# Feed-forward matmuls over 512 tokens at a time, with the two hidden weight matrices streamed through a ring of four slices

## The chip, the core and the metric

The kernel runs on one NeuronCore of a Trainium2 chip. A core has five engines that run side by side and meet only through semaphores: TensorE (PE in the profile; its weight loads are PEld), VectorE (DVE), ScalarE (ACT), GpSimd (POOL) and SyncE (SP), which here only issues transfers. The metric is the device time of one execution in microseconds (us); less is better.

## The reference

Eight batches of 512 tokens with 256 features pass through four residual blocks: a state-space layer (called ssm below), a feed-forward, a delta-rule attention (delta below) and the same feed-forward again with the same weights.

```python
def _L0_ffn_ref(x, w1_w, w1_s, w2_w, w2_s, h1_w, h1_s, h2_w, h2_s, w3_w, w3_s):
    h = jax.nn.silu(_tlin(x, w1_w, w1_s)) * _tlin(x, w2_w, w2_s)      # 256 -> 1024
    h = jax.nn.gelu(_tlin(h, h1_w, h1_s), approximate=False)          # 1024 -> 1024
    h = jax.nn.gelu(_tlin(h, h2_w, h2_s), approximate=False)          # 1024 -> 1024
    return _tlin(h, w3_w, w3_s)                                       # 1024 -> 256
...
x = x + ssm(_layernorm(x))
x = x + ffn(_layernorm(x))
x = x + delta(_layernorm(x))
x = x + ffn(_layernorm(x))
```

The weights of the feed-forward are -1, 0 or 1 with one scale per output; `_tlin` is a matmul and that scale. The ssm layer is computed in four chunks of 128 tokens, the delta layer in four tiles of 128 tokens, each of four blocks of 32.

## The kernel before

**Feed-forward.** One pass is one feed-forward of one batch; there are sixteen, numbered p. The weights have the type fp32r, and each activation is split into two fp32r parts, hi and lo (`hA_hi`, `hA_lo`, `hB_hi`, `hB_lo`, `xf_hi`, `xf_lo`), so each weight block is multiplied twice. A pass has two units of 256 tokens (`TOK`), one after the other. Of a unit, TensorE makes: the first layer in 8 slices (line 1259: w1 and w2 beside each other in one PSUM bank, 256 columns each), two hidden layers of 4 slices each (line 1279: two blocks of 128 outputs side by side in one bank), the transposes of the normed input of the next unit (line 1243, called xt below), and the last layer (line 1301, w3). Two banks `F` alternate.

**Around it.** After a first-layer slice, ScalarE does silu into `gate` (line 709), VectorE multiplies (line 939) and rounds to the hi part (line 943), and GpSimd subtracts to get the lo part (line 588). After a hidden slice ScalarE does two gelus (lines 713 and 714) and the hi part (line 717), and GpSimd the lo part. A bank is free again after the last engine has read it: for the first layer that is VectorE's line 939, behind ScalarE's silu. All h1 and h2 weights (`h1_sb`, `h2_sb`, 4 MB each) lie in SBUF, loaded once at the start.

**Order.** Each engine has one fixed list of instructions, made by `window`: the attention's generator (ssm or delta) and the feed-forward's are advanced in turns, and a table such as `BODY_PLAN["pe"]` says how many feed-forward pieces (each ends at a `yield`) follow each attention piece. A TensorE piece is 8 matmuls of the first layer, 12 or 20 of a hidden layer, 16 of w3, or the transposes. The program is: ssm(0) alone; FIRST (ssm(1) with pass 0); PEEL (delta(0), ssm(2), one and a half passes); BODY, a hardware loop of five iterations (delta(b-1), ssm(b+1), two passes); LATE; LAST (delta(7) with pass 14); and pass 15 alone.

**Stages of a BODY iteration**, as TensorE goes through them. D1: projections and Gram matrices of the delta layer, four tiles. Solve: VectorE inverts 32x32 triangles in 31 dependent steps (lines 1127 and 1129) while TensorE has only feed-forward work; then the result goes through DRAM (`t_scr`) into `tbd`, which GpSimd clears first. Walk: 16 dependent blocks, each TensorE line 1504, VectorE line 1155, TensorE lines 1516 and 1521, VectorE line 1161, and back to TensorE 1504. Ssm: four chunks of the state-space layer.

## Time and profile before

| | us |
|---|---|
| median of 3 runs | 2550.48 (2546.01 to 2552.0) |
| the profiled execution, its own time | 2549.43 |
| its span | 2547.7 |
| busy in it: PE / DVE / ACT / POOL | 2259.9 / 1361.7 / 1118.6 / 843.0 |
| one BODY iteration | 300.4 |
| of it D1 / solve and round trip / walk / ssm | 45.9 / 60.2 / 65.5 / 128.8 |
| from the end of the last walk to the end | 104.3 |

The page of the profile gives for each engine the time in which it had an instruction in execution. On TensorE that overlaps: a matmul of the feed-forward is recorded with 0.28 us but the next one starts 0.117 us later. So the pace is read from starts, not from durations.

### The profile page before, as it was taken

The numbers are of one execution on the slowest core, as the hardware profiler recorded it, in microseconds if no ns is written. First come the engines' busy times: TensorE is split into PE (matmuls) and PEld (weight loads), VectorE is DVE, ScalarE is ACT, GpSimd is POOL, SyncE is SP. The second block draws the span as 40 slices with busy tenths as digits, with TensorE's granted clock in tenths as the row PEclk, the third lists the DMA queues.
The fourth block names the chain that finished last, engine by engine and source line by source line (L and its number), as shares of the span: only waits on it lengthen the run. The fifth ranks groups of instructions, "written<-read, shape, count | busy, mean of one in ns | idle before, by whom it ended". The sixth has DMA issues, their size and how long they took to land.

```text
span 2547.7 us, 61597 instructions
## 1 busy us (share of the span) xinstructions
PE 2259.9 (89%) x25057; PEld 2016.0 (79%) x25088; DVE 1361.7 (53%) x3348; ACT 1118.6 (44%) x2160; POOL 843.0 (33%) x1003
## 2 busy tenths in 40 slices
PE   4679988887999989999989988999899998898888
PEld 3558877776888878888888878888788887897888
DVE  4555374456735656466645657356663756546531
ACT  3347332452335733365334743357333663333323
POOL 3123332323333333332333333342333433233233
PEclk8779999997999999999999999999999999999999
DMA  7000000000010001000010000100010000000000
GB/s 252 1 1 1 1 18 18 1 1 3 24 28 2 1 19 30 7 1 2 18 33 4 1 3 18 35 2 1 7 32 17 1 2 18 24 5 18 17 11 9
DMA packets 85468, 43.84 MB, mean 17 GB/s; under 512 B 69936, under 2 KB 80048, under 8 KB 85168
## 3 DMA queue, kind: packets, MB, share of 16 engines
q1 hardware_dynamic: 81504, 28.11, 4.4%
q0 software_dynamic: 3664, 11.53, 1.4%
q8 instruction: 212, 3.47, 0.6%
q14 instruction: 88, 0.72, 0.1%
HBM read 27.05 MB, written 12.58 MB: 16 GB/s over the span
## 4 chain that ended last, share of the span: by engine, by line
PE 60%; DVE 22%; issue 8%; POOL 5%; DMA 2%; ACT 2%; DVEq 0%; SPq 0%; POOLq 0%; ACTq 0%
PE F L1279 27%; PE Q L1338 5%; PE F L1259 5%; DVE ti L1129 4%; DVE prod L1127 3%; PE F L1301 2%; PE Q L1395 2%; PE Q L1409 2%; PE Q L1372 2%; POOL hA_lo L588 2%; DVE hid L939 2%; PE Q L1436 2%; POOL rn L640 2%; PE Q L1504 2%; PE Q L1350 1%
## 5 line engine op out<-in xcount | busy, mean ns | idle before, releaser
L588 POOL TENSOR_TENSOR hA_lo<-hid,hA_hi 128x256 fp32r<-128x256 f32 (+1 forms) x384 | 358.4, 935 | 712.7 <-ACT hA_hi L717 406.4
L1279 PE MATMUL F<-hA_hi,h_sb 128*128 128x256 f32 x2048 | 506.9, 289 | 7.6 <-DVEq L942 4.8
L1279 PE MATMUL F<-hB_hi,h_sb 128*128 128x256 f32 x2048 | 501.2, 287 | 3.2 <-POOL hB_lo L588 3.2
L1279 PE MATMUL F<-hA_lo,h_sb 128*128 128x256 f32 x2048 | 489.9, 280 | 0.0
L1279 PE MATMUL F<-hB_lo,h_sb 128*128 128x256 f32 x2048 | 486.3, 279 | 0.0
L1279 PEld LDWEIGHTS F<-hA_hi,h_sb 128*128 128x128 f32 x2048 | 387.8, 189 | 19.3 <-DVEq L942 5.8
L1279 PEld LDWEIGHTS F<-hB_hi,h_sb 128*128 128x128 f32 x2048 | 384.9, 188 | 14.0 <-POOL hB_lo L588 5.4
L1279 PEld LDWEIGHTS F<-hA_lo,h_sb 128*128 128x128 f32 x2048 | 388.2, 190 | 1.7 <-issue 1.4
L1279 PEld LDWEIGHTS F<-hB_lo,h_sb 128*128 128x128 f32 x2048 | 386.3, 189 | 0.5 <-issue 0.5
L1259 PE MATMUL F<-xf_hi,w_sb 128*128 128x256 f32 x1024 | 277.2, 306 | 80.6 <-DVEq L942 57.0
L713 ACT ACTIVATE hid<-F,sh_sb 128x256 f32<-128x256 f32 x256 | 121.4, 474 | 397.6 <-PE F L1279 395.9
L588 POOL TENSOR_TENSOR hB_lo<-hid,hB_hi 128x512 fp32r<-128x512 f32 x128 | 167.0, 1305 | 354.2 <-ACT hB_hi L717 354.1
L1259 PEld LDWEIGHTS F<-xf_hi,w_sb 128*128 128x128 f32 x1024 | 198.6, 194 | 105.8 <-DVEq L942 72.4
L1259 PE MATMUL F<-xf_lo,w_sb 128*128 128x256 f32 x1024 | 256.8, 286 | 0.0
L709 ACT ACTIVATE gate<-F,s_sb 128x256 f32<-128x256 f32 x256 | 120.3, 477 | 243.6 <-PE F L1259 209.7
L1259 PEld LDWEIGHTS F<-xf_lo,w_sb 128*128 128x128 f32 x1024 | 199.5, 195 | 0.5
L939 DVE SCALAR_TENSOR_TENSOR hid<-F,s_sb,gate 128x256 f32<-128x256 f32 x256 | 122.6, 479 | 62.1 <-ACT gate L709 52.0
L1301 PE MATMUL F<-w_sb,hA_hi 128*128 128x256 f32 x512 | 135.8, 302 | 10.3 <-ACTq L716 6.0
L1338 PE MATMUL Q<-win_sb,xT 128*128 128x512 f32 (+1 forms) x384 | 134.2, 500 | 3.4 <-ACT xT L729 3.4
L1129 DVE TENSOR_TENSOR ti<-ti,prod 128x31 f32<-128x31 f32 (+15 forms) x248 | 130.6, 526 | 8.5
L1155 DVE STREAM_TRANSPOSE ur<-Q 128x64 f32<-128x64 f32 x128 | 31.4, 245 | 187.4 <-PE Q L1504 186.9
L1301 PE MATMUL F<-w_sb,hA_lo 128*128 128x256 f32 x512 | 129.1, 288 | 0.0
...
## 6 DMA issues: line engine op xcount, KB each, us to landing
h_sb<-h_dram POOLq DMA_DIRECT2D x2, 4096.0 KB, 23.8
x_sb<-x_dram SPq DMA_DIRECT2D x8, 512.0 KB, 4.3
...
au<-a_scr SPq DMA_DIRECT2D x8, 512.0 KB, 3.3
t_scr<-ti SPq DMA_DIRECT2D x8, 512.0 KB, 2.6
tbd<-t_scr SPq DMA_DIRECT2D x128, 32.0 KB, 1.9
out_dram<-x_sb SPq DMA_DIRECT2D x8, 512.0 KB, 3.0
...
```

The source lines that it names most:

```text
L588: pool.tensor_tensor(lo, hid[:, n % 2, 0:w, :], hi.bitcast(F32), ALU.subtract).then_inc(f_lo.handle, 1)
L640: pool.tensor_tensor(rn[:], srow[:], neg_half[:], ALU.pow).then_inc(d_rn.handle, 1)
L709: act.activation(gate[:, n % 2, :], ps[:, 0:TOK], ACT.Silu, scale=s1_sb[:, j:j + 1]).then_inc(f_act.handle, 1)
L713: act.activation(hid[:, n % 2, 0, :], ps[:, 0:TOK], ACT.Gelu, scale=scales[:, k:k + 1])
L939: own(dve.scalar_tensor_tensor(hid[:, n % 2, 0, :], bank_of(s)[:, TOK:2 * TOK], s2_sb[:, j:j + 1], gate[:, n % 2, :], ALU.mult, ALU.mult))
L1127: own(dve.tensor_tensor(pr, bcast(ti[:, 0:j + 1, j], 2, below), bcast(au[:, j, j + 1:BLK], 1, j + 1), ALU.mult))
L1129: own(dve.tensor_tensor(rest, rest, pr, ALU.subtract))
L1259: last = pe.matmul(ps[:, i * TOK:(i + 1) * TOK].rearrange("p (t n) -> p t n", t=2), w[:, k, j * P:(j + 1) * P], part[:, :, k, :], start=(k ...
L1279: last = pe.matmul(ps[:, i * TOK:(i + 1) * TOK], w[:, k, o:o + P], part[:, k, :], start=(i == 0 and k == 0 and part is src[0]), stop=(i == ...
L1301: last = pe.matmul(ps[:, t * D:(t + 1) * D], part[:, k, t * P:(t + 1) * P], w3_sb[:, k, :], start=(k == 0 and part is hA_hi), stop=(k == K ...
L1338: last = pe.matmul(Q[q][:, 0:c1 - c0], xT[:, k, :], win_sb[:, k, c0:c1], start=(k == 0), stop=(k == 1))
L1372: pe.matmul(Q[5][:, h * HP:(h + 1) * HP], seg[:, h, :], xdt[:, h, :], start=True, stop=True)
```

## The change

- A pass is no longer cut into units of 256 tokens. Every matmul of the first and of the hidden layers has 512 columns, and so has every operation on ScalarE, VectorE and GpSimd behind them. w1 and w2 of a slice go into a bank each: ScalarE frees the one, VectorE the other. A pass has 8 + 8 first-layer slices of 4 matmuls, 16 hidden slices of 16, two transposes, and w3 as before.
- The wider activations take the room of `h1_sb` and `h2_sb`. In their place is `h_sb`, a ring of four slices of 512 KB. When TensorE is through with hidden slice m, GpSimd issues the load of slice m + 4 into its place, 16 loads per pass. They come from `h_scr`, a copy of h1 and h2 in DRAM that lies slice by slice; 16 transfers on SP make it at the start, and GpSimd waits for them before pass 0.
- The halves that BODY is cut at are other ones: `parts` instead of `units`. Part 0 is the first layer and hidden layer one (32 pieces), part 1 hidden layer two, both transposes and w3 (22 pieces). Pieces of a hidden layer are 8 matmuls, those of the first layer 4.
- Since both transposes of the next pass stand ahead of w3, all four tiles of the next input have to be normed by then; before it was two of them.
- All five tables of numbers are new.

```diff
-HSLICES = KT + KT // 2 + KT // 2
+HSLICES = 3 * KT
+H_SLICE = 2 * KT
+XT_SLICE, W3_SLICE = 4 * KT, 4 * KT + UNITS
+RING = 4
...
 BODY_PLAN = {
-    "pe": ("2 1 2 0 0 0 2 0 0 1 0 1 0 1 1 1 30 1 1 1 1 0 1 0 0 1 1 1 0 0 1 1 1 1 0 2 0 2 0 0 2 1 1 2 0 1 1 "
+    "pe": ("2 1 3 0 0 0 1 1 0 0 1 1 0 0 2 1 41 1 1 0 1 0 0 0 0 1 0 1 0 0 0 0 1 0 0 1 0 0 0 0 0 0 1 0 0 2 0 "
...
-        h1_sb = sb("h1_sb", [P, KT, HID], F32R)
-        h2_sb = sb("h2_sb", [P, KT, HID], F32R)
+        h_sb = sb("h_sb", [P, RING, KT, P], F32R)
...
+            for m in range(2 * KT):
+                sp.dma_start(h_flat(m), h_dram(m)).then_inc(h_copied, 16)
...
+            for m in range(RING):
+                pool.dma_start(ring_slice(m), h_dram(m)).then_inc(f_w[m].handle, 16)
...
+                        if n >= KT and (n - KT + RING < 2 * KT or more):
+                            m = n - KT
+                            yield n - 0.5
+                            pool.wait_ge(f_ps.handle, f_ps.at(p, H_SLICE + m + 1))
+                            pool.sem_inc(pool_gate, 1)
+                            pool.dma_start(ring_slice(m), h_flat((m + RING) % (2 * KT))).then_inc(f_w[m % RING].handle, 16)
...
+            def hidden_layer(p, layer):
+                src = ((hA_hi, hA_lo), (hB_hi, hB_lo))[layer]
+                for j in range(KT):
+                    m = layer * KT + j
+                    yield H_SLICE + m
+                    pe.wait_ge(f_w[m % RING].handle, f_w[m % RING].at(p, loaded(m)))
+                    ps = bank(p, H_SLICE + m)
+                    for k in range(KT):
+                        if k == KT // 2:
+                            yield H_SLICE + m + 0.5
...
+                        for h in src:
+                            last = pe.matmul(ps[:], ring_slice(m)[:, k, :], h[:, k, :], start=(k == 0 and h is src[0]),
+                                             stop=(k == KT - 1 and h is src[1]), skip_group_check=True)
+                    last.then_inc(f_ps.handle, 1)
```

What the tables do is seen in the order of instructions. The rows below are in program order, with the kernel's own line numbers; ISA and REGISTER_ALU rows are waits and their arithmetic.

VectorE in the solve of a BODY iteration, before: the steps of the solve (`prod`, `ti`) with the first-layer work (`hid`, then `hA_hi`) of 256 tokens between them, in the last third of the 31 steps.

```order
813 L1127 TENSOR_TENSOR prod<-ti,au 128x207
814 L1129 TENSOR_TENSOR ti<-ti,prod 128x23x9
815 L937 REGISTER_ALU
816 L938 REGISTER_ALU
817 L939 SCALAR_TENSOR_TENSOR hid<-F,s_sb,gate 128x256
818 L943 CAST hA_hi<-hid 128x256
819 L937 REGISTER_ALU
820 L938 REGISTER_ALU
821 L939 SCALAR_TENSOR_TENSOR hid<-F,s_sb,gate 128x256
822 L943 CAST hA_hi<-hid 128x256
823 L1127 TENSOR_TENSOR prod<-ti,au 128x192
824 L1129 TENSOR_TENSOR ti<-ti,prod 128x24x8
```

The same place on VectorE, now:

```order
731 L1148 TENSOR_TENSOR prod<-ti,au 128x207
732 L1150 TENSOR_TENSOR ti<-ti,prod 128x9x23
733 L959 REGISTER_ALU
734 L960 REGISTER_ALU
735 L961 REGISTER_ALU
736 L962 SCALAR_TENSOR_TENSOR hid<-F,s_sb,gate 128x512
737 L966 CAST hA_hi<-hid 128x512
738 L959 REGISTER_ALU
739 L960 REGISTER_ALU
740 L961 REGISTER_ALU
741 L962 SCALAR_TENSOR_TENSOR hid<-F,s_sb,gate 128x512
742 L966 CAST hA_hi<-hid 128x512
```

The eight first-layer slices moved to the first third of the solve (steps 7 to 11), each twice as wide; both w3 halves and a transpose's lo part stand in the first six steps too, and steps 12 to 31 follow without a feed-forward instruction.

TensorE in the walk of a BODY iteration, before: between lines 1521 and 1504 or between 1504 and 1516 there are feed-forward matmuls (`F`) nearly everywhere, here after both.

```order
2750 L1279 MATMUL F<-hB_hi,h_sb 128x256
2751 L1279 MATMUL F<-hB_lo,h_sb 128x256
2752 L1512 REGISTER_ALU
2753 L1516 MATMUL Q<-ur,kr 32x32 x8
2754 L1521 MATMUL Q<-pc,ur 32x32 x8
2755 L1504 MATMUL Q<-kqT,st 32x64 x8
2756 L1279 MATMUL F<-hB_hi,h_sb 128x256
```

The walk on TensorE, now (L1531, L1543 and L1548 are the lines 1504, 1516 and 1521 of before):

```order
1854 L1531 MATMUL Q<-kqT,st 32x64 x8
1855 L1539 REGISTER_ALU
1856 L1543 MATMUL Q<-ur,kr 32x32 x8
1857 L1548 MATMUL Q<-pc,ur 32x32 x8
1858 L1509 MATMUL Q<-ident,oT 128x128 x2
1859 L1531 MATMUL Q<-kqT,st 32x64 x8
1860 L1539 REGISTER_ALU
1861 L1543 MATMUL Q<-ur,kr 32x32 x8
1862 L1548 MATMUL Q<-pc,ur 32x32 x8
1863 L1531 MATMUL Q<-kqT,st 32x64 x8
1864 L1295 MATMUL F<-hB_hi,h_sb 128x512
```

Of 364 feed-forward matmuls in 31 places between the first and the last block of a BODY walk, 80 wide ones in 10 places are left; the other places stand open, one attention instruction behind the other.

GpSimd, hidden layer in the solve of a BODY iteration, before:

```order
230 L588 TENSOR_TENSOR hB_lo<-hid,hB_hi 128x512
231 L645 MEMSET tbd 128x1024
232 L646 MEMSET st 128x64
233 L588 TENSOR_TENSOR hB_lo<-hid,hB_hi 128x512 x3
234 L588 TENSOR_TENSOR hA_lo<-hid,hA_hi 128x512 x4
```

And now:

```order
306 L603 DMA h_sb<-h_scr 128x1024
307 L609 ISA
308 L611 TENSOR_TENSOR hB_lo<-hid,hB_hi 128x512
309 L601 REGISTER_ALU
310 L603 DMA h_sb<-h_scr 128x1024
311 L609 REGISTER_ALU
312 L611 TENSOR_TENSOR hB_lo<-hid,hB_hi 128x512
```

Ahead of each subtraction stands the issue of a load, with a wait of its own for the matmuls of that slice.

## Rows read from the trace of the kernel before

**Rows 1.** The page: busy time, TensorE's clock in 40 slices, chain by engine

```profile
PE 2259.9 (89%) x25057; PEld 2016.0 (79%) x25088; DVE 1361.7 (53%) x3348; ACT 1118.6 (44%) x2160; POOL 843.0 (33%) x1003
...
PEclk8779999997999999999999999999999999999999
...
PE 60%; DVE 22%; issue 8%; POOL 5%; DMA 2%; ACT 2%; DVEq 0%; SPq 0%; POOLq 0%; ACTq 0%
```

**Rows 2.** Windows (start:end us, length, busy us by engine, PEclk, DMA share, GB/s)

```profile
core 0: us, PE busy (x) PEld busy (x) DVE busy (x) ACT busy (x) POOL busy (x), PEclk, DMA share, GB/s
...
1204.50:1250.40 45.90, 38.71 (x457) 30.90 (x457) 26.97 (x77) 15.76 (x42) 16.44 (x17) 0.96 0.07 12
1250.40:1310.60 60.20, 53.39 (x457) 50.81 (x458) 38.71 (x88) 21.94 (x43) 21.46 (x21) 1.00 0.11 32
1310.60:1376.10 65.50, 64.17 (x1208) 57.16 (x1207) 24.11 (x77) 21.72 (x44) 20.81 (x27) 1.00 0.07 16
1376.10:1504.80 128.70, 119.78 (x1022) 107.31 (x1022) 79.40 (x178) 82.61 (x145) 44.97 (x56) 1.00 0.01 1
2398.10:2443.40 45.30, 39.83 (x989) 34.25 (x987) 16.59 (x55) 9.82 (x22) 9.57 (x13) 0.89 0.06 10
2443.40:2547.70 104.30, 91.31 (x762) 87.94 (x758) 22.39 (x53) 36.92 (x70) 34.19 (x36) 0.97 0.03 11
```

**Rows 3.** Groups by line: count, busy, mean ns, idle before and its releaser

```profile
L1279 PE MATMUL F<-hA_hi,h_sb 128*128 128x256 f32 x2048 | 506.9, 289 | 7.6 <-DVEq L942 4.8 <-POOL hA_lo L588 2.6
L1259 PE MATMUL F<-xf_hi,w_sb 128*128 128x256 f32 x1024 | 277.2, 306 | 80.6 <-DVEq L942 57.0 <-DVEq L963 8.4 <-issue 8.4
```

**Rows 4.** Timeline of TensorE, hidden layer in one stretch: start us, recorded length

```profile
1003.32 0.28 PE L1279 MATMUL F<-hA_lo,h_sb 128*128 128x256 f32 x1
...
1004.61 0.28 PE L1279 MATMUL F<-hA_hi,h_sb 128*128 128x256 f32 x1
```

**Rows 5.** Timeline of TensorE: sixteen 64-column records, then 512-column records of the ssm projection

```profile
1122.76 1.98 PE L1372 MATMUL Q<-xdt,seg 128*128 128x64 f32 x16
1124.67 1.11 PE L1376 MATMUL Q<-hst,cT 64*128 64x64 f32 x16
...
1115.11 1.02 PE L1338 MATMUL Q<-win_sb,xT 128*128 128x512 f32 x2
...
1117.68 0.59 PE L1338 MATMUL Q<-win_sb,xT 128*128 128x512 f32 x1
```

**Rows 6.** Timeline of TensorE in the LAST walk: a block with nothing between its steps

```profile
2408.97 0.31 PE L1521 MATMUL Q<-pc,ur 32*32 32x32 f32 x16
2409.55 0.42 PE L1504 MATMUL Q<-kqT,st 32*32 32x64 f32 x16 [0.27 <-issue]
2410.43 0.30 PE L1516 MATMUL Q<-ur,kr 32*32 32x32 f32 x13 [0.46 <-DVE ur L1155]
2410.58 0.30 PE L1521 MATMUL Q<-pc,ur 32*32 32x32 f32 x15
```

**Rows 7.** Timeline, solve of a BODY iteration: VectorE, GpSimd and SP

```profile
1256.70 0.74 DVE L1127 TENSOR_TENSOR prod<-ti,au 128x31 f32<-128x31 f32 x1 [4.90 <-DMA au<-a_scr]
1257.47 0.19 DVE L1129 TENSOR_TENSOR ti<-ti,prod 128x31 f32<-128x31 f32 x1
...
1259.83 1.34 POOL L588 TENSOR_TENSOR hB_lo<-hid,hB_hi 128x512 fp32r<-128x512 f32 x1 [2.44 <-ACT hB_hi L717]
...
1260.07 1.28 DVE L1127 TENSOR_TENSOR prod<-ti,au 128x156 f32<-128x156 f32 x1
...
1261.38 0.32 DVE L1129 TENSOR_TENSOR ti<-ti,prod 128x156 f32<-128x156 f32 x1
...
1299.16 0.22 DVE L1129 TENSOR_TENSOR ti<-ti,prod 128x31 f32<-128x31 f32 x1
...
1303.57 1.80 SPq L499 DMA_DIRECT2D tbd<-t_scr  x4
```

**Rows 8.** Timeline of GpSimd and DMA issues (KB each, us to landing): what loads cost

```profile
16.84 1.78 POOL L557 DMA_DIRECT2D h_sb<-h_dram  x2
...
h_sb<-h_dram POOLq DMA_DIRECT2D x2, 4096.0 KB, 23.8
x_sb<-x_dram SPq DMA_DIRECT2D x8, 512.0 KB, 4.3
```

**Rows 9.** Groups by line on VectorE, ScalarE and GpSimd: what one operation takes

```profile
L939 DVE SCALAR_TENSOR_TENSOR hid<-F,s_sb,gate 128x256 f32<-128x256 f32 x256 | 122.6, 479 | 62.1 <-ACT gate L709 52.0 <-DVE ti L1129 4.2 <-DVE x_sb L965 1.9
L943 DVE CAST hA_hi<-hid 128x256 fp32r<-128x256 f32 x256 | 93.1, 364 | 37.7 <-DVE hid L939 10.5
L588 POOL TENSOR_TENSOR hB_lo<-hid,hB_hi 128x512 fp32r<-128x512 f32 x128 | 167.0, 1305 | 354.2 <-ACT hB_hi L717 354.1 <-POOL st L646 0.2
L717 ACT CAST hA_hi<-hid 128x512 fp32r<-128x512 f32 x128 | 79.4, 620 | 14.6 <-ACT hid L714 0.4
```

More of the change, by code:

```diff
@@ L713, in ffn @@
[L713 to L720 removed]
+                        scales = (sh1_sb, sh2_sb)[part]
@@ L722, in ssm_stage @@
+                        own(act.activation(hid[:, n % 2, :], bank_of(s)[:], ACT.Gelu, scale=scales[:, m % KT:m % KT + 1]))
+                        act.sem_inc(f_freeA.handle, 1)
+                        act.copy(ffn_dst(n)[0], hid[:, n % 2]).then_inc(f_hiA.handle, 1)
+                    if part == 1 and more:
+                        for u in range(UNITS):
+                            yield XT_SLICE + u
+                            xt_high(p, XT_SLICE + u, u)
             def ssm_stage(b, p):
@@ L837, in _ @@
             alone(ssm_stage(0, 0))
-            xt_high(0, -1)
+            for u in range(UNITS):
+                xt_high(0, u - UNITS, u)
             window(ssm_stage(1, 1), ffn(0, 0), FIRST_PLAN["act"])
@@ new lines, in first_layer @@
+            def first_layer(p):
+                for j in range(KT):
+                    for i, w in enumerate((w1_sb, w2_sb)):
+                        yield 2 * j + i
+                        if j == 0 and i == 0:
+                            pe.wait_ge(f_xlo.handle, f_xlo.at(p, UNITS))
+                        ps = bank(p, 2 * j + i)
+                        for k in range(2):
+                            for x in (xf_hi, xf_lo):
+                                last = pe.matmul(ps[:].rearrange("p (t n) -> p t n", t=NT), w[:, k, j * P:(j + 1) * P],
+                                                 x[:, :, k, :], start=(k == 0 and x is xf_hi),
+                                                 stop=(k == 1 and x is xf_lo))
+                        last.then_inc(f_ps.handle, 1)
@@ new lines, in last_layer @@
+            def last_layer(p, u, more):
+                s = W3_SLICE + u
+                for t in range(2):
+                    yield s + 0.5 * t
+                    if t == 0:
+                        if more:
+                            ps = bank(p, s)
+                        else:
+                            pe.wait_ge(f_freeA.handle, f_freeA.at(p, 2 * KT - UNITS + u + 1))
+                            ps = bank_of(s)
+                    o = (2 * u + t) * P
+                    for k in range(KT):
+                        if t == 0 and u == 0:
+                            pe.wait_ge(f_lo.handle, f_lo.at(p, 2 * KT + k + 1))
+                        for h in (hA_hi, hA_lo):
+                            last = pe.matmul(ps[:, t * D:(t + 1) * D], h[:, k, o:o + P], w3_sb[:, k, :],
+                                             start=(k == 0 and h is hA_hi), stop=(k == KT - 1 and h is hA_lo))
+                last.then_inc(f_ps.handle, 1 if more or u else 1 + UNITS)
@@ new lines, in ffn @@
+            def ffn(p, b, more=True, parts=range(PARTS)):
+                if 0 in parts:
+                    yield from first_layer(p)
+                    yield from hidden_layer(p, 0)
+                if 1 in parts:
+                    yield from hidden_layer(p, 1)
+                    if more:
+                        for u in range(UNITS):
+                            yield XT_SLICE + u
+                            xt(bank(p, XT_SLICE + u), p + 1, u)
+                    for u in range(UNITS):
+                        yield from last_layer(p, u, more)
@@ L1534, in _ @@
             alone(ssm_stage(0, 0))
-            xt(0, -1, 0, 0)
-            pe.wait_ge(wr_dma, 16 * 5)
+            for u in range(UNITS):
+                xt(bank_of(u - UNITS), 0, u)
+            pe.wait_ge(wr_dma, 16 * 3)
             pe.wait_ge(wd_dma, 16)
```

319 lines of the change are left out of this document (132 added, 187 removed), and 62 rows, old and new, of tables (BODY_PLAN, FIRST_PLAN, LAST_PLAN, LATE_PLAN).

## The prediction

> **What bounds the kernel now.** I read the page first [rows 1]: TensorE is busy for 89% of the span and holds 60% of the chain of waits; no other engine is over 53%. Next the windows of one BODY iteration [rows 2]: in solve, walk and ssm TensorE's idle time is 6.8, 1.3 and 8.9 us of 60.2, 65.5 and 128.7, so the length of these stages is the TensorE work put into them. Only D1 (7.2 idle of 45.9) is partly paced by a chain across engines. Then the pace of that work, from starts in the timeline: 11 steps from 1003.32 to 1004.61 [rows 4] are 0.1173 us for each 256-column matmul of the feed-forward. A BODY iteration has 1280 such in the first and hidden layers, 150 us of 300.4, and 128 of w3, 15 us.
>
> Is that pace the columns or something per matmul? Sixteen records with 64 columns and full 128x128 weights start 1.91/16 = 0.119 us apart [rows 5]: as slow with a quarter of the columns, so 0.117 is a floor per matmul, not the price of 256 columns. Six steps of 512-column f32 records take 2.57 us, 0.428 each [rows 5]; such a matmul is written as two records and an f32 one needs more array time than an fp32r one: 256 fp32r columns fit under 0.117, so an fp32r column costs at most 0.46 ns where an f32 record's costs 0.84. The nearest row thus gives half of 0.428, **0.2145 us for a 512-column fp32r matmul**; the other end is twice the floor, 0.2346, no gain. I take 0.2145, since the f32 records show that the array can take 512 columns without a gap, and nothing in the trace shows fp32r columns slower.
>
> The Trainium skill, page "TensorE: Matmul & The Clock Gate", sections "Back-to-back issue gap" and "LDWEIGHTS", prices a warm matmul at N/2.4 + 2.5 ns and a weight load at 128/1.2 = 107 ns; by that page 256 columns would take 109 ns, where the rows show 117, and 512 would take 216. By it the first term below would be 5120 x (0.2346 - 0.2158) = 96 us instead of 103.
>
> **Part 1: wider matmuls.** 8192 hidden and 2048 first-layer matmuls [rows 3] (x2048 is one of four hidden groups, x1024 one of two of the first layer) become 5120. Saved TensorE work: 5120 x (0.2346 - 0.2145) = **103 us**, 12.9 in each batch's two passes; w3 stays. It counts where TensorE sets the end, so I go through the stages of a BODY iteration with what the new table puts in each.
>
> - **D1, 45.9 us.** Before 128 matmuls (12 pieces), 15.0 us. Now 13 pieces of hidden layer two, 104 x 0.2145 = 22.3. That is +7.3; the idle 7.2 can take some, and no first-layer work waits for VectorE here now. I take +3 (ends 0 and +7).
> - **Solve and round trip, 60.2 us.** TensorE now has 224 wide matmuls (48.0), all 64 of w3 (7.5) and two transposes (1.2): 56.8 us, less than 60.2. So the end is set by VectorE. Counted from the last Gram record: the eight first-layer slices follow 3 hidden pieces (5.2), transposes (1.2) and w3 (7.5) at 1.72 us each, so VectorE is through with them at 29.3; with operations of about 0.75 and 0.62 (0.479 and 0.364 for half the columns [rows 9]) it keeps that pace. Twenty solve steps are then left. An operation takes 0.19 us for 31 columns and 0.32 for 156 [rows 7], so 0.158 + 0.00104 per column, and 0.04 between two; the twenty have 3850 columns: 2 x (20 x 0.158 + 4.0) + 1.6 = 15.9. And an operation that meets a GpSimd subtraction is held: 1.28 instead of 0.32 at 1260.07, beside the one at 1259.83 [rows 7]. Seven or eight such, 7 us. The solve ends at 52, where before it ended at 49; the shortest round trip is 8 us (1299.38 to the issue of `tbd` at 1303.57, 1.80 long, and about 2 to land). GpSimd clears `tbd` only when the solve is done, and the last slices' subtractions queue behind that, so TensorE loses a little. I take a walk that starts at 64: **+4** (ends 0 and +8).
> - **Walk, 65.5 us.** A block with nothing in it takes 0.58 + 0.88 + 0.15 = 1.61 us [rows 6]; sixteen, with the three stretches that form the next tile and the transposes, about 30.6. Before, 364 matmuls in 31 places add 34.9: 1.13 each, of 1.38 us of matmuls, so 0.25 of each hides. Now ten places with 8 x 0.2145 = 1.72 us cost 1.47 each: 30.6 + 14.7 = 45.3. The LAST walk of before, with 148 feed-forward matmuls, took 45.3 too, and its clock was 0.89 of full, a mix of 2.4 and 1.2 GHz, where the filled BODY walk has 1.00 [rows 2]. With 0.7 for the clock: 46, **-19.5**. Most of this is work that moved to D1 and the solve, not a gain of its own.
> - **Ssm, 128.8 us.** Before about 500 matmuls, 58.7 us; now 232 wide and 64 of w3, 57.3. The first layer's waits, 80.6 us in all, 57.0 of them for VectorE to release a bank [rows 3], shrink, since ScalarE alone now frees every other bank: -1 here. **-2.5**.
>
> Sum for an iteration -15 us, five of them **-75**. It is a little more than 12.9: the rest is waits of the first layer, against more idle time in the walk.
>
> **Part 2: the other stages**, by the same prices. FIRST (one pass, 6.4 us of matmuls less, fewer waits): -8. PEEL: its solve has only hidden work and no first-layer operation on VectorE, its walk fewer pieces, its ssm more: -12. LATE: like BODY, D1 +3, solve +4, walk -16: -8. LAST and pass 15: of 104.3 us after the last walk [rows 2], 722 matmuls were 85; now 24 wide ones and 64 of w3 from pass 14 and a pass of 320 and 64 are 88.9, and overheads stay: +2. The walk loses 9 pieces: -9. The solve without VectorE's first-layer work: -7. Together -14.
>
> **Part 3: the ring.** 256 loads, one more issue on GpSimd ahead of each subtraction. An issue there took 1.78/2 = 0.89 us [rows 8]. It starts when the matmuls end, as ScalarE's gelu and hi part do (about 0.69 + 0.62), and the subtraction waits for these anyway: **hidden, 0**; if the cover is gone, 0.89 for each of 16 hidden slices of a pass that TensorE has to wait for. A load of 512 KB landed in 4.3 us from SP, and 4096 KB on GpSimd's queue in 23.8 us beside others [rows 8]; TensorE needs the slice three slices later, 3 x 3.43 = 10.3 us. Hidden too. The copy of h1 and h2 lies in the 146 us of ssm(0): I take +1 for the crowd at the start (ends 0 and +5).
>
> The Trainium skill, "SBUF — State Buffer", section "Who interferes with whom", says that VectorE and GpSimd share a port pair as an exclusive lock, and that a transfer issued from GpSimd has to write its descriptors through it. The hold of 1.0 us above agrees; no row shows an issue beside a busy VectorE.
>
> **Sum.** -75 - 8 - 12 - 8 - 14 + 1 = -116 against the profiled execution's own 2549.43: 2433.4. The median stands 1.05 above that execution: **2434.5 us**.
>
> **Rivals.**
> - **A: the 512 columns run at twice the floor.** For it: the only fp32r pace in the trace is 0.117 for 256. Against: rows 5. Then the 103 us are gone and the moved work stays: 2434.5 + 103 = 2537, or 2500 where half is lost.
> - **B: the issues are not hidden.** GpSimd holds VectorE for each issue as for a subtraction, in solve and D1, where the chain runs over VectorE: 10 issues x 0.9 us in each of 8 batches, +72: 2506.
> - **C: slower than before.** The walks and the round trips leave TensorE short of work, and its clock falls to 1.2 GHz there and in the stages behind. At the start, with TensorE sparsely fed, the clock is 0.7 to 0.8 [rows 1], in the LAST walk 0.89. It costs 0.2145 us for each wide matmul run at the low level. The change loses from the point where about 540 of 5120, or 14.5 us in each batch, are eaten up by that; if a whole walk and a third of the work in D1 and solve ran at 1.2 GHz, 20 to 22 us a batch are lost: 2600. Against: D1 and solve are fuller than before.
> - **D: the streaming saves work that was waiting time anyway**; the idle time grows by what is saved: 2550.
>
> **Chances.** Forecast (2395 to 2480) 0.62; A or B and their mixtures (2480 to 2545) 0.20; better than 2395, where the solve's end doesn't move, 0.03; D 0.03; C 0.12. The range takes the forecast's case and most of A and B: **2395 to 2535**. A measurement of this kernel can tell about 0.2% (5 us) from no change: faster 0.85, same 0.03, slower 0.12.
>
> **What the profile after will show.** Starts of `h_sb` matmuls 0.2145 apart, or 0.235 (A). A BODY iteration of 285 us: D1 49, solve with round trip 64, walk 46, ssm 126. First-layer idle well under 80 us. If issues on GpSimd stretch VectorE's solve operations, B. If PEclk has 7s and 8s in the walks and behind, C. A wait of TensorE for `h_sb<-h_scr` would say that the ring is too short. What would upset it all: a wait at a place that the tables filled before, in D1 above all, where 7 us of matmuls were added to a chain.

## The result, and the profile after

The changed kernel is slower: median 2571.53 us over 12 runs (2558.74 to 2577.97), against 2551.36 (2545.41 to 2552.84) for the kernel before on the same chip. The ratio is **1.0079, 95% interval 1.0063 to 1.0096**. The forecast was 2434.5 with a range of 2395 to 2535, so the time lies outside, and on the other side of zero. The profiled execution took 2572.26 us, its span is 2570.5.

First the page of the changed kernel: busy time, TensorE's clock in 40 slices, the chain by engine. They answer to [rows 1].

```profile
PE 2265.9 (88%) x19937; PEld 1753.3 (68%) x19968; DVE 1382.7 (54%) x3092; ACT 973.5 (38%) x1719; POOL 963.5 (37%) x1129
...
PEclk8779998899999999999999999999999999999989
...
PE 59%; DVE 23%; issue 8%; POOL 4%; DMA 3%; ACT 2%; SPq 1%; DVEq 0%; POOLq 0%; ACTq 0%
```

TensorE has 5120 fewer matmul instructions and is busy for 6 us more. So the work did not get less. The windows are the stages of [rows 2]: D1, solve with round trip, walk and ssm of the third BODY iteration, then the LAST walk and the end.

```profile
core 0: us, PE busy (x) PEld busy (x) DVE busy (x) ACT busy (x) POOL busy (x), PEclk, DMA share, GB/s
1207.30:1260.90 53.60, 47.72 (x425) 34.62 (x425) 25.22 (x60) 16.24 (x40) 22.14 (x22) 0.90 0.28 76
1260.90:1336.20 75.30, 65.97 (x332) 50.89 (x328) 43.62 (x89) 22.52 (x33) 30.91 (x31) 0.98 0.33 97
1336.20:1385.50 49.30, 43.09 (x960) 31.37 (x959) 17.05 (x56) 8.96 (x17) 12.87 (x19) 0.92 0.27 73
1385.50:1519.10 133.60, 125.41 (x785) 100.12 (x786) 87.23 (x182) 74.15 (x126) 52.88 (x67) 0.97 0.13 40
2420.40:2458.90 38.50, 26.53 (x887) 19.61 (x886) 15.33 (x54) 4.57 (x10) 6.44 (x11) 0.79 0.12 27
2458.90:2570.50 111.60, 102.89 (x482) 83.06 (x482) 22.81 (x41) 33.06 (x49) 43.20 (x44) 0.96 0.25 76
```

These windows and those of [rows 2] are not cut at the same marks. Here D1 begins where the last output projection of the ssm layer ends, and the walk ends with its last block. [rows 2] begin D1 2.1 us earlier, where that projection starts, and end the walk 3.0 us earlier, ahead of the last block (the LAST walk 2.4 us). At the marks used here the kernel before reads (the solve is as in [rows 2]):

```profile
1206.60:1250.40 43.80, 36.74 (x450) 29.47 (x449) 25.09 (x73) 15.68 (x41) 15.99 (x16) 0.96 0.07 12
...
1310.60:1379.10 68.50, 67.17 (x1260) 59.98 (x1260) 25.59 (x79) 21.72 (x44) 21.68 (x27) 1.00 0.07 15
1379.10:1507.10 128.00, 118.77 (x974) 105.93 (x978) 79.98 (x180) 82.88 (x145) 44.66 (x56) 1.00 0.01 1
2398.10:2445.80 47.70, 42.23 (x1036) 36.51 (x1034) 17.08 (x57) 9.82 (x22) 9.57 (x13) 0.89 0.05 9
2445.80:2547.70 101.90, 88.92 (x724) 85.68 (x710) 21.90 (x52) 36.92 (x70) 34.19 (x36) 0.97 0.03 11
```

All stages below go by these marks. The iteration takes 311.8 us for 300.5. The walk got shorter as forecast, all other stages of the iteration got longer, and the clock fell in every one of them. The five BODY iterations together take 1552.7 us for 1497.5, where the forecast had 75 less; all the rest of the program takes 1017.8 for 1050.2, with a forecast of 41 less. So the loss lies in BODY. Two kinds of row show what the forecast had not seen. The pace, in the timeline of TensorE in the solve, where the clock is full (answers to [rows 4]):

```profile
1303.69 0.40 PE L1295 MATMUL F<-hA_hi,h_sb 128*128 128x512 f32 x1
...
1306.26 0.39 PE L1295 MATMUL F<-hA_lo,h_sb 128*128 128x512 f32 x1
```

Eleven steps in 2.57 us are **0.2336 us a matmul**, twice the 0.117 of 256 columns. And GpSimd beside VectorE in D1, third tile (timelines of both engines):

```profile
1240.58 0.43 DVE L1121 TENSOR_TENSOR k_sb<-k_sb,rn 128x256 f32<-128x256 f32 x1 [0.40 <-POOL rn L664]
1241.04 5.31 DVE L1122 TENSOR_TENSOR uw<-k_sb,sig 128x256 f32<-128x256 f32 x1
...
1240.50 0.62 POOL L603 DMA_DIRECT2D h_sb<-h_scr  x1
1241.14 1.29 POOL L611 TENSOR_TENSOR hA_lo<-hid,hA_hi 128x512 fp32r<-128x512 f32 x1
1242.38 0.58 POOL L603 DMA_DIRECT2D h_sb<-h_scr  x1
1242.98 1.28 POOL L611 TENSOR_TENSOR hA_lo<-hid,hA_hi 128x512 fp32r<-128x512 f32 x1
1244.19 0.57 POOL L603 DMA_DIRECT2D h_sb<-h_scr  x1
1244.79 1.27 POOL L611 TENSOR_TENSOR hA_lo<-hid,hA_hi 128x512 fp32r<-128x512 f32 x1
```

GpSimd had stood behind two `rn` whose inputs came late; three ring issues and three subtractions were queued and ran in a row. VectorE's `uw`, of 0.42 us, started 0.1 us before the end of the first issue and ended 0.3 us after the last subtraction: 5.31 us. It is the third of the four tiles, and the same hold stands in each of the five BODY iterations (5.30 to 5.33 us) and nowhere else. TensorE's transposes of that tile wait for it, and what follows them runs at a lower clock:

```profile
1246.41 0.69 PE L1456 MATMUL Q<-ident,q_sb 128*128 128x128 f32 x2 [3.90 <-DVE uw L1122]
...
1247.74 4.70 PE L1463 MATMUL Q<-wqkvb_sb,xTd 128*128 128x512 f32 x8
```

At the end of the solve TensorE waits for the round trip, 2.90 us in this iteration. The second line has all such waits (us in total, times, longest); the kernel before has one, of 0.8 us:

```profile
1331.95 0.65 PE L1495 MATMUL Q<-tbd,uw 128*32 128x128 f32 x16 [2.90 <-DMA tbd<-t_scr]
...
PE Q L1495 <- DMA tbd<-t_scr: 18.4, 8, 4.4
```

### The profile page after: what moved, and what is told of

The parts are those of the page before. It is cut to its first block, busy times and chain, and to the rows that moved or that the text cites. A ratio compares the mean times of both kernels' runs of the same rounds, so it can differ in the third digit from the quotient of the medians.

```text
span 2570.5 us, 50857 instructions
## 1 busy us (share of the span) xinstructions
PE 2265.9 (88%) x19937; PEld 1753.3 (68%) x19968; DVE 1382.7 (54%) x3092; ACT 973.5 (38%) x1719; POOL 963.5 (37%) x1129
## 4 chain that ended last, share of the span: by engine, by line
PE 59%; DVE 23%; issue 8%; POOL 4%; DMA 3%; ACT 2%; SPq 1%; DVEq 0%; POOLq 0%; ACTq 0%
PE F L1295 23%; PE F L1316 5%; PE Q L1365 5%; PE F L1275 5%; DVE ti L1150 5%; DVE prod L1148 4%; PE Q L1422 3%; DVE hid L962 2%; PE Q L1463 2%; PE Q L1531 2%; PE Q L1399 2%; PE Q L1543 2%; DMA tbd<-t_scr 2%; PE Q L1436 2%; PE Q L1377 1%
## 5 line engine op out<-in xcount | busy, mean ns | idle before, releaser
L611 POOL TENSOR_TENSOR hA_lo<-hid,hA_hi 128x512 fp32r<-128x512 f32 x256 | 331.1, 1294 | 402.4 <-DVE hA_hi L966 355.2
L1295 PE MATMUL F<-hB_hi,h_sb 128*128 128x512 f32 x1024 | 441.8, 431 | 7.9 <-POOL hB_lo L611 7.9
L1295 PE MATMUL F<-hB_lo,h_sb 128*128 128x512 f32 x1024 | 423.0, 413 | 0.0
L1295 PE MATMUL F<-hA_hi,h_sb 128*128 128x512 f32 x1024 | 411.4, 402 | 1.2 <-POOL hA_lo L611 0.6
L1295 PE MATMUL F<-hA_lo,h_sb 128*128 128x512 f32 x1024 | 405.8, 396 | 0.0
L1275 PE MATMUL F<-xf_hi,w_sb 128*128 128x512 f32 x512 | 222.0, 434 | 53.6 <-DVEq L965 42.0
L1295 PEld LDWEIGHTS F<-hB_lo,h_sb 128*128 128x128 f32 x1024 | 204.6, 200 | 43.5
L1295 PEld LDWEIGHTS F<-hA_hi,h_sb 128*128 128x128 f32 x1024 | 192.8, 188 | 49.9 <-POOL hA_lo L611 1.1
L1295 PEld LDWEIGHTS F<-hA_lo,h_sb 128*128 128x128 f32 x1024 | 193.0, 188 | 44.0
L1275 PE MATMUL F<-xf_lo,w_sb 128*128 128x512 f32 x512 | 204.3, 399 | 0.0
L1316 PE MATMUL F<-w_sb,hA_hi 128*128 128x256 f32 x512 | 128.1, 291 | 10.9 <-POOL hA_lo L611 7.7
## 6 DMA issues: line engine op xcount, KB each, us to landing
a_scr<-amv SPq DMA_DIRECT2D x32, 128.0 KB, 2.3
```

What stands on the lines that cost most here:

```text
L611: pool.tensor_tensor(lo, hid[:, n % 2, :], hi.bitcast(F32), ALU.subtract).then_inc(f_lo.handle, 1)
L1275: last = pe.matmul(ps[:].rearrange("p (t n) -> p t n", t=NT), w[:, k, j * P:(j + 1) * P], x[:, :, k, :], start=(k == 0 and x is xf_hi), st ...
L1295: last = pe.matmul(ps[:], ring_slice(m)[:, k, :], h[:, k, :], start=(k == 0 and h is src[0]), stop=(k == KT - 1 and h is src[1]), skip_gro ...
L1316: last = pe.matmul(ps[:, t * D:(t + 1) * D], h[:, k, o:o + P], w3_sb[:, k, :], start=(k == 0 and h is hA_hi), stop=(k == KT - 1 and h is h ...
```

## Experiments

All ratios are against the kernel before, run on the same chip. "Back" is what a variant gives back of the changed kernel's 1.0079, in us of 2549: (1.0079 - ratio) x 2549.

### 1. What a matmul costs

Behind the last pass:

```diff
+            for _ in range(2):
+                run(24, lambda i: h_sb[:, i % RING, ...], lambda i: hB_hi[:, i % KT, :])       # 512; then 384, 320, 256, 128
+                ...
+                run(24, lambda i: BFv(h_sb[...])[:, 0:P], lambda i: BFv(hB_hi[...])[:, 0:512])  # bf16; then 256
+                run(8, lambda i: win_sb[...], lambda i: xnf[...])                               # f32
```

> The changed kernel with 432 more matmuls on TensorE behind its last pass, in groups of one form (results unused): fp32r with full 128x128 weights and 512, 384, 320, 256 and 128 columns, then 512 columns with the same weights every time, then the same operands read as bf16 with 512 and 256 columns, then f32 with 512. Theory (fp32r columns cost 0.455 ns each at the full granted clock, over a floor of 0.117 us per matmul): 512: 0.233, 384: 0.175, 320: 0.146, 256: 0.117, 128: 0.11 to 0.117; same weights 0.233. Rival (a column costs 0.417 ns and each matmul 0.02 us more, for its weights): 384: 0.180, 320: 0.153, 256: 0.127. If the width of the fp32r operand sets the price, bf16 with 512 columns runs at 0.213 to 0.217; if it is the array or the clock, bf16 takes 0.233 too. The time of the kernel: 2572 + some 65 us.

Of this kernel there is one execution, and only its trace is used. In the timeline of TensorE a row is n matmuls, so its length less one record (0.39 us for 512 fp32r columns, 0.28 for 256) is n - 1 steps; the profile calls fp32r operands f32:

```profile
2561.26 1.56 PE L1591 MATMUL Q<-hB_hi,h_sb 128*128 128x512 f32 x6
...
2567.31 1.55 PE L1591 MATMUL Q<-hB_hi,h_sb 128*128 128x384 f32 x8
...
2574.43 1.45 PE L1591 MATMUL Q<-hB_hi,h_sb 128*128 128x256 f32 x11
...
2577.00 0.83 PE L1591 MATMUL Q<-hB_hi,h_sb 128*128 128x128 f32 x6
...
2586.36 1.46 PE L1591 MATMUL Q<-hB_hi,h_sb 128*128 128x512 bf16 x6
...
2588.30 1.46 PE L1591 MATMUL Q<-hB_hi,h_sb 128*128 128x512 bf16 x8
...
2589.27 1.47 PE L1591 MATMUL Q<-hB_hi,h_sb 128*128 128x256 bf16 x12
...
2590.36 1.47 PE L1591 MATMUL Q<-hB_hi,h_sb 128*128 128x256 bf16 x12
```

fp32r: 0.234 for 512 columns, 0.166 to 0.181 for 384 (its own record lies between the two; rows with six steps between their starts are 1.04 us apart, 0.173), 0.147 for 320, 0.117 for 256, 0.11 for 128. bf16, from starts nine and ten steps apart (2586.36 and 2588.30, 2589.27 and 2590.36): 0.216 for 512 columns and 0.109 for 256. With the same weights every time 512 fp32r columns still take 0.233. So from 256 columns up an fp32r column costs 0.455 ns and a bf16 column about 0.42. Half the columns of 256 save only 0.007 us, so 0.11 is about the least for a matmul with full fp32r weights, and 256 columns lie just above it. There is nothing per matmul to save: the price is in the columns and hangs on the type of the operands, and the rival with 0.02 us per matmul falls.

### 2. What the pace is worth

```diff
+COLS = 472
-  last = pe.matmul(ps[:], ring_slice(m)[:, k, :], h[:, k, :], ...
+  last = pe.matmul(ps[:, 0:COLS], ring_slice(m)[:, k, :], h[:, k, 0:COLS], ...   # first layer likewise
```

> The changed kernel with only 472 of 512 columns in every matmul of the first and hidden layers (the last 10 tokens of each tile, or the last 40 of the batch, are left out of them; everything else as it is). A matmul then takes 472 x 0.455 ns = 0.2148 us, which is what the prediction gave the one with 512 columns. If the pace is the step that failed and TensorE sets the end as the prediction has it, 5120 x 0.0185 = 95 us are the most that can come back, and 60 to 85 are expected, the rest lost to waits in the solve: 2490 to 2510. If waits of VectorE and round trips set the end now, under 35 come back: over 2537.

2528.79 us, ratio 0.9917 (0.9893 to 0.9942): **41 us back**, between the two expectations (60 to 85, under 35) and nearer to the lower. With the forecast's own price per matmul the kernel is only 0.8% faster than before. Under half of the 95 us of TensorE work sat on the path; the other 54 turned into waits, which is rival D's mechanism.

### 3. What the ring is worth

```diff
-                            pool.wait_ge(f_ps.handle, f_ps.at(p, H_SLICE + m + 1))
-                            pool.sem_inc(pool_gate, 1)
-                            pool.dma_start(ring_slice(m), h_flat((m + RING) % (2 * KT))).then_inc(f_w[m % RING].handle, 16)
...
-                    pe.wait_ge(f_w[m % RING].handle, f_w[m % RING].at(p, loaded(m)))
+                    pe.wait_ge(f_w[m % RING].handle, 16)
```

> The changed kernel without the 252 reloads of the ring: GpSimd issues none, and all hidden slices are multiplied with the four slices loaded first (so the hidden layers compute something else). Theory (the ring costs only through the landing of tbd and au beside its traffic, 2 to 3 us in each of 8 batches): 15 to 25 us faster, 2547 to 2557, the landing of tbd back from 2.5 to 1.9 us and its last one in a BODY iteration from 5.5 to 3.4. Rival B (the issues hold VectorE and delay the subtractions): 50 us or more faster. If the ring is hidden as predicted: within 5 us of 2571.

2483.99 us, ratio 0.9749 (0.9718 to 0.9779): **84 us back**, far more than my theory gave. This is the largest single cause. The same four stages without reloads:

```profile
1171.70:1217.80 46.10, 43.68 (x425) 32.13 (x425) 22.50 (x60) 16.25 (x40) 18.41 (x15) 1.00 0.06 10
1217.80:1288.90 71.10, 64.70 (x328) 50.14 (x328) 43.63 (x89) 22.45 (x33) 25.31 (x21) 1.00 0.09 28
1288.90:1335.40 46.50, 41.04 (x960) 29.88 (x959) 15.81 (x56) 8.58 (x17) 9.58 (x13) 0.96 0.10 21
1335.40:1465.30 129.90, 123.37 (x784) 98.77 (x786) 87.08 (x182) 74.55 (x126) 46.62 (x57) 0.99 0.00 1
```

D1 is 7.5 us shorter, the solve 4.2, the walk 2.8, ssm 3.7. The clock is back at 1.00 in D1 and the solve and at 0.96 in the walk, with nothing added there.

### 4. Bytes or issues

```diff
-  pool.dma_start(ring_slice(m), h_flat((m + RING) % (2 * KT)))...
+  pool.dma_start(ring_slice(m)[:, 0:2], h_flat((m + RING) % (2 * KT))[:, 0:2])...
```

> The changed kernel with every reload of the ring cut to two of a slice's eight blocks, 128 KB for 512 KB; GpSimd issues as many as before (the other six blocks keep older weights, so the hidden layers compute something else). Theory from the run without reloads, which gave back 87 us, and from VectorE's 5.32 us operation beside three issues and three subtractions of GpSimd in D1: the issues are what costs. Then three quarters of the bytes give back only what the landings of tbd and au cost, 2 to 3 us a batch: 2548 to 2560. Rival (the traffic of 137 MB is what costs): 50 us or more come back, under 2520.

2535.24 us, ratio 0.9952 (0.9935 to 0.9969): 32 us back, between the two expectations. So both cost. With a quarter of the bytes the small `tbd` transfers land in 2.0 us for 2.5 and `au` in 3.6 for 4.4 (before: 1.9 and 3.3), and the solve stage takes 71.2 us for 75.3, as without any reload (71.1), and in neither of the two runs TensorE waits for `tbd`. The 5 us holds in D1 stay, as the group of `uw` shows, here with 128 KB loads:

```profile
L1122 DVE TENSOR_TENSOR uw<-k_sb,sig 128x256 f32<-128x256 f32 x32 | 38.1, 1189 | 1.1
```

Without reloads the mean of these 32 operations is 574 ns for 1189, in the kernel before 437.

### 5. The order on GpSimd

```diff
-                            pool.dma_start(...)            # ahead of the subtraction
                         pool.tensor_tensor(lo, hid[:, n % 2, :], hi.bitcast(F32), ALU.subtract)...
+                        pool.dma_start(...)                # behind it
```

> The changed kernel with each of GpSimd's ring issues behind the subtraction that it stands ahead of. If it is the delay of the subtraction (0.6 us issue and 0.45 us behind it, with TensorE waiting for the lo part) that costs, 15 to 40 us come back. If it is the hold on VectorE by issues and subtractions back to back, the same trains remain and the time stays within 10 us of 2571.

2544.23 us, ratio 0.9984 (0.9965 to 1.0002): 24 us back with all bytes and issues kept, and the kernel level with the one before. The gain is in D1: in the mean of the five BODY iterations it takes 46.3 us for 52.6, the solve 74.8 for 75.7. `k_sb` and `uw` in the same place are held over one subtraction each:

```profile
1227.02 1.51 DVE L1119 TENSOR_TENSOR k_sb<-k_sb,rn 128x256 f32<-128x256 f32 x1 [0.42 <-POOL rn L662]
1228.56 1.84 DVE L1120 TENSOR_TENSOR uw<-k_sb,sig 128x256 f32<-128x256 f32 x1
...
1226.96 1.28 POOL L607 TENSOR_TENSOR hA_lo<-hid,hA_hi 128x512 fp32r<-128x512 f32 x1
1228.20 0.61 POOL L610 DMA_DIRECT2D h_sb<-h_scr  x1
1228.83 1.27 POOL L607 TENSOR_TENSOR hA_lo<-hid,hA_hi 128x512 fp32r<-128x512 f32 x1
1230.04 0.58 POOL L610 DMA_DIRECT2D h_sb<-h_scr  x1
...
1231.16 2.77 PE L1461 MATMUL Q<-wqkvb_sb,xTd 128*128 128x512 f32 x8
```

In the third iteration D1 is 7.2 us shorter. Of that, 0.7 is the wait for the lo part at its start (1.1 for 1.8), the delay that the expectation named. The shorter hold gives 2.4. The other 4.1 is TensorE's clock behind the two waits: the 16 matmuls behind the first take 4.0 us for 5.5, and transposes and projection behind the second 3.4 for 6.0 (the projection alone 2.77 for 4.70). So neither cause that the expectation set apart stands alone, and the clock takes more than either.

The same six instructions still run back to back. Why a train that begins with an issue holds VectorE to its end, and one that begins with a subtraction lets it through, is not settled.

Experiments 4 and 5 together part the ring's cost by stage: fewer bytes give back what the solve lost and leave D1 at 51.5 us (mean of five); the other order gives back D1 and leaves the solve. What the walk and ssm lost, 4.7 us of 16.1 in the mean iteration, neither explains fully.

### 6. The same loads in the kernel before

```diff
+  pool.wait_ge(f_ps.handle, f_ps.at(p, u * SLICES + j + 1))
+  pool.wait_ge(dummy_in.handle, ...)                 # the transfer before; second form: the fourth before
+  pool.dma_start(dummy[q % KT], h1[...]).then_inc(...)
```

> The kernel before, with one 512 KB transfer from DRAM to DRAM (contents unused) issued by GpSimd ahead of each of the 16 hidden subtractions of a pass, at the places where the changed kernel reloads its ring. Theory (issues on GpSimd hold VectorE, here as there): 40 to 90 us slower than before, 2590 to 2640. Rival (the 87 us hang on the changed kernel's order, where several issues and subtractions stand back to back): under 20 us.

2667.41 us, ratio 1.0448 (1.0409 to 1.0488), over what was expected; GpSimd stood 307 us behind its own landings, so the number is that of my added wait too.

> As e8_before_load, but an issue waits for the landing of the fourth transfer before it, as in the changed kernel, not of the last one, behind which GpSimd stood for 307 us. Theory (256 issues and their traffic cost the same 87 us in either kernel): 2600 to 2640 in place of 2667. Rival (they cost by where they stand in the changed kernel's order): under 2575.

With the wait four transfers back: 2609.46, ratio 1.0232 (1.0212 to 1.0253), **59 us**. So a load of 512 KB per hidden slice is dear in the old order as well. But not by the mechanism that the theory named, and its number came out right by luck. Holds on VectorE hardly grew (`uw` 515 ns in the mean for 437), and of the BODY iteration only the solve got longer:

```profile
1276.70:1344.00 67.30, 57.31 (x455) 54.44 (x453) 38.15 (x88) 21.95 (x43) 26.66 (x31) 0.92 0.37 115
```

67.3 for 60.2, with D1 at 43.3, walk at 68.5 and ssm at 128.1 as before. The inverse is done 1 us later than before, the round trip behind it takes 17.3 us for 11.2, and TensorE waits 31.0 us for `tbd` in all. These transfers write to DRAM, not to SBUF, so the 59 is a neighbour of the 84, not the same price.

### 7. The clock

```diff
+                def filler():
+                    pe.matmul(Q[5], w1_sb[:, 0, 0:P], w1_sb[:, 0, 0:512], start=True, stop=True)
                         last.then_inc(d_ws.handle, 1)
+                        filler()                           # and behind the group of line 1548
```

> The changed kernel with one more 512-column matmul (result unused) on TensorE behind each of the two groups of small matmuls in every block of the walks, 32 in a walk, so that TensorE isn't left with 32-column work alone. If the low granted clock of the walk and of the stages behind costs what rival C says, the walk and the ssm stage come back to 1.00 and the kernel gets 15 to 40 us faster in spite of the added work. If the clock costs little, the added 32 x 0.233 = 7.5 us a walk hide only in its 6.2 us of idle time, and the kernel gets 10 to 35 us slower.

2584.60 us, ratio 1.0137 (1.0098 to 1.0175): 15 us slower than the changed kernel. D1 and walk of the same iteration:

```profile
1210.60:1262.40 51.80, 45.25 (x426) 32.97 (x425) 25.21 (x60) 16.25 (x40) 22.18 (x22) 0.97 0.29 80
...
1337.80:1389.30 51.50, 49.96 (x991) 34.69 (x990) 18.10 (x56) 9.71 (x18) 13.46 (x20) 1.00 0.26 70
```

The clock rose from 0.92 to 1.00 in the walk and from 0.90 to 0.97 in D1. D1 is 1.8 us shorter, the walk 2.2 longer with its added matmuls. Over the five BODY iterations the two are level (1553.6 us for 1552.7); the 15 us arose outside them. So filling the walk doesn't pay. It doesn't show that the low clock is cheap: the waits of D1 and the low clock behind them stayed (0.93 to 0.97 in the five D1), and experiment 5 found 4.1 us of it in one D1.

### 8. Both causes at once

Experiments 2 and 3 together.

> Both at once, 472 of 512 columns in the first and hidden layers (40 tokens of a batch left out there) and no reloads of the ring (the hidden layers compute something else). If pace and ring are two causes that add up, 2571 - 43 - 87 = 2441, and with the forecast's own price of a matmul and its free ring the forecast, 2434.5, should come out within 15 us: 2425 to 2450. If they share waits (whoever is late hides the other), less than 110 come back: over 2460. If the pace is worth more once VectorE isn't held, under 2420.

**2439.66 us**, ratio 0.9574 (0.9556 to 0.9591): 129 us back, 41 + 84 = 125. The two causes add up, and with both taken away the kernel lies 5 us over the forecast. That it lies so near is in part luck: its five BODY iterations take 1445.9 us, 23 over their forecast, and the rest of the program 990.0, 19 under.

### 9. A version that is faster than both

```diff
-        hA_lo = sb("hA_lo", [P, KT, L], F32R)                 # hB_lo, xf_lo likewise
+        hA_lo = sb("hA_lo", [P, KT, L], BF16)
+        def top(w):                                          # upper halves of fp32r weights
+            return w.bitcast(BF16).rearrange("p (n e) -> p n e", e=2)[:, :, 1]
-  last = pe.matmul(ps[:], ring_slice(m)[:, k, :], h[:, k, :], ...
+  last = pe.matmul(ps[:], top(wk) if h is src[1] else wk, h[:, k, :], ...
```

> The changed kernel with the lo parts of the activations (the residue behind the fp32r hi part) kept as bf16 and multiplied with the upper halves of the same fp32r weights, which hold -1, 0 and 1 exactly. In the forms measured in e1_forms a bf16 matmul with 512 columns runs at 0.216 us and an fp32r one at 0.233. 2560 wide matmuls x 0.017 + 1024 of w3 x 0.009 = 53 us less TensorE work; by the share that came back with 472 columns (43 of 95) 25 us faster: 2540 to 2555. If TensorE sets the end everywhere: 2520. If the strided weight load or the conversions cost, over 2571.

2572.37, ratio 1.0086 (1.0057 to 1.0115): nothing gained. fp32r and bf16 matmuls alternate here, and a pair takes 0.4625 us (0.231 each), not 0.216 + 0.233 = 0.449.

```diff
+        h8_sb = sb("h8_sb", [P, 2 * KT, KT, P], mybir.dt.float8e4)
-                            pool.dma_start(ring_slice(m), h_flat(...))...
+            def unpack(m):                                   # on ScalarE, behind the hi part of slice m - 4
+                act.copy(ring_slice(m), h8_sb[:, m % (2 * KT)]).then_inc(f_w[m % RING].handle, 1)
```

> As e11_bf16lo, and h1 and h2 no longer come from DRAM: all 16 slices lie in SBUF as 8-bit floats (16 KB of a partition, -1, 0 and 1 exactly), and ScalarE, behind the hi part of hidden slice m, widens slice m + 4 into the ring. GpSimd issues nothing for the ring. Theory (issues cost 87 us, ScalarE has the time at 38% busy): 2571 - 25 - 87 + 0 to 30 for ScalarE's 252 copies of about 1.1 us each, which lie ahead of its work for the attention: 2460 to 2490, faster than both kernels. Rival (ScalarE becomes what D1, solve or ssm waits for): over 2530.

2556.18, ratio 1.0046 (1.0022 to 1.0070), neither expectation. The BODY iterations were at 300.9 us for 310.5 in the mean, but ssm(0) ended some 32 us late: GpSimd issued 16 strided loads first and reached its first rsqrt at 53 us.

```diff
-            alone(ssm_stage(0, 0))
+            for m, _ in enumerate(ssm_stage(0, 0)):
+                if 1 <= m <= KT: ...                         # two of the 16 loads a piece
-  for k in range(KT): for h in src: ...
+  for h in src: for k in range(KT): ...                      # hi blocks, then lo blocks; all but the first slice
```

> As e12_packed, with two changes: GpSimd's 16 first loads of h1 and h2 are spread over ssm(0), two a piece (in e12_packed they held back its first rsqrt until 53 us and the end of ssm(0) by about 32 us), and TensorE takes the hi blocks of a slice together and then the lo blocks (alternating fp32r and bf16 ran at 0.2312 us a matmul in e11_bf16lo, where 0.225 is the mean of the two forms alone). 2556 - 32 for the start, - 10 to 20 of 2560 x 0.006 = 16 and less: 2505 to 2525, faster than the kernel before by over 1%. If the start wasn't the loads: over 2540.

**2495.05 us**, ratio 0.9785 (0.9769 to 0.9801): 2.2% faster than the kernel before, 2.9% faster than the changed one, and under the expected 2505. Grouped by type, the matmuls of the hidden layers start 0.234 (fp32r) and 0.216 us (bf16) apart. ScalarE's 256 copies, of 1.04 us each, cost little, but not nothing: the five BODY iterations take 1479.8 us, where those without reloads took 1472.0 with fp32r alone.

```profile
L723 ACT CAST h_sb<-h_sb 128x1024 fp32r<-128x1024 fp8e4 x256 | 266.2, 1041 | 0.0
```

## Why the prediction was wrong

| us | before | forecast | after | no reloads | no reloads, 472 columns |
|---|---|---|---|---|---|
| D1 | 43.8 | 46.8 | 53.6 | 46.1 | 44.5 |
| solve and round trip | 60.2 | 64.2 | 75.3 | 71.1 | 69.7 |
| walk | 68.5 | 49.0 | 49.3 | 46.5 | 45.8 |
| ssm | 128.0 | 125.5 | 133.6 | 129.9 | 127.1 |
| the third BODY iteration | 300.5 | 285.5 | 311.8 | 293.6 | 287.1 |
| all five | 1497.5 | 1422.5 | 1552.7 | 1472.0 | 1445.9 |
| the rest of the span | 1050.2 | 1009.2 | 1017.8 | 1007.4 | 990.0 |

All columns go by the marks of the profile after; the forecast is the kernel before with the prediction's own changes (+3, +4, -19.5, -2.5, and -75 and -41 in all).

- **The pace, "I take 0.2145".** The step that failed is the one from [rows 5]: that f32 records take 512 columns in 0.428 for two shows what the array can do with f32, and nothing of fp32r. The halved f32 record is the pace of bf16 (0.216), not of fp32r. The 64-column records are f32 ones as well, and as slow as 256 fp32r columns by chance: the least for an fp32r matmul is 0.11, and 256 columns cost 0.1165 by themselves. So "0.117 is a floor per matmul, not the price of 256 columns" was wrong: it is their price. The bound 0.2346 was right, rival A was the truth, and "nothing in the trace shows fp32r columns slower" was no reason, since nothing showed them as fast. The page "TensorE: Matmul & The Clock Gate" of the Trainium skill, section "Back-to-back issue gap", gives no fp32r price: by its formula 512 columns take 216 ns, which bf16 meets here (0.216) and fp32r does not (0.234). The section calls that formula the one of an isolated matmul and gives 131 ns for 512 columns in a stream of weight loads and matmuls; the prediction left that out, and no form here came near it. Price of the step: 5120 x 0.019 = 97 us of work, 41 of them on the path by experiment 2.
- **The ring, "hidden, 0".** The other failed step, worth 84 us. Its working looked at one subtraction behind one issue, and there it was right: in the solve an issue at 1267.27 ends before ScalarE's hi part is there. It left out what is queued when GpSimd comes late, that 132 MB (252 loads of 512 KB) travel beside transfers on which the chain waits, and that TensorE's clock falls behind such waits. Of the 84, 32 came back with three quarters of the bytes gone, by the solve above all, and 24 with the issue moved behind the subtraction, by D1; what the other 28 are stays open. "TensorE needs the slice three slices later" was right: no wait for `h_sb<-h_scr` appears.
- **The solve, "at 1.72 us each".** The third failed step. Neither cause explains that VectorE's inverse ended 61.2 us behind the last Gram record, with reloads and without (60.7 with 472 columns), for a forecast of 52. The eight first-layer slices took from 1277.3 to 1299.2, 2.7 us each: 8 us more than forecast, and they began 2.5 later. The round trip behind the inverse took 14.0 us, 9.9 without reloads, for a forecast of 12. VectorE and its waits there (timeline after):

```profile
1282.34 1.33 DVE L1150 TENSOR_TENSOR ti<-ti,prod 128x192 f32<-128x192 f32 x1
1283.97 0.75 DVE L962 SCALAR_TENSOR_TENSOR hid<-F,s_sb,gate 128x512 f32<-128x512 f32 x1 [0.30 <-PE F L1275]
...
1294.94 0.75 DVE L962 SCALAR_TENSOR_TENSOR hid<-F,s_sb,gate 128x512 f32<-128x512 f32 x1 [0.86 <-PE F L1275]
1295.84 0.43 DVE L966 CAST hA_hi<-hid 128x512 fp32r<-128x512 f32 x1
1297.13 0.75 DVE L962 SCALAR_TENSOR_TENSOR hid<-F,s_sb,gate 128x512 f32<-128x512 f32 x1 [0.86 <-PE F L1275]
```

  Even with nothing between, a slice takes 2.19 us. The second bank is always w2's, and TensorE can fill it again only when VectorE has read it: multiply 0.75, then four matmuls, then the next multiply. The forecast counted that ScalarE frees every other bank as a gain and did not follow the one that it doesn't free. A solve step between two slices meets their subtraction and adds 1.1 more. No run tested this by itself; it is read from these rows. The idle time of the first layer did shrink, 53.6 us in the group of `xf_hi` for 80.6 [rows 3].
- **The walk, -19.5.** Right: 68.5 became 49.3 with both causes, 46.5 without reloads. The LAST walk lost 9.2 us for a forecast of 9, though its clock, 0.79, fell lower than 0.89.
- **The clock, "0.7 for the clock".** Allowed for in the walk alone. In D1 it fell from 0.96 to 0.90, and 0.10 of 53.6 us is 5 us at most (an estimate); experiment 5 shows 4.1 of it.
- **Outside BODY** the forecast was too careful: 990.0 us without both causes for 1009.2. Of the 19 us, 16 lie ahead of the first BODY iteration, where FIRST and PEEL were given -20 without rows of their own. In BODY it was 23 too hopeful, most of it in the solve.
- **The sums.** Four slips, each small. The slices' 29.3 us has terms for 27.7 and none for the other 1.6; LATE's terms +3, +4 and -16 make -9, not -8; the matmuls behind the last walk go from 85 to 88.9, entered as +2; half of 103 lost is 2486, not 2500. And 21 solve steps were left behind the slices, not twenty.
- **Rivals.** A was right about the pace. Its time, 2537, has two errors that partly cancel: all 103 us on the path, where 41 were, and a free ring. B's 72 us lie near 84, in part by luck: it priced each issue at 0.9 us in solve and D1, but the inverse ends at the same time with the issues and without, and what costs is one train in D1, the bytes beside the round trip, and the clock behind both. A and B have to be added: 2434.5 + 41 + 84 = 2560, 12 under the result. C gave the right sign. Its clock took 4.1 of 7.2 us in one D1; over the whole kernel its share was not measured. D as a whole is out, but of the 95 us of work in experiment 2, 54 were waiting time. The prediction's own last warning came true: a wait in D1, where matmuls had been added to a chain.
- **The chances.** A and B, each within its own price, were held for alternatives and given 0.20 together. They are independent, so the case of both belonged in the sum, and with it a time near or over 2550.

On the lock: the Trainium skill, page "SBUF — State Buffer", section "Who interferes with whom", says that a VectorE instruction with two SBUF inputs contends with a GpSimd instruction that reads SBUF. The holds over one subtraction agree: 1.51 us for 0.43 and 1.84 for 0.42 in experiment 5. One operation held over three subtractions, 5.31 us, is more than that sentence covers.
